# Two graph layers on one core: layer 2's probabilities turned by the transposing DMA instead of TensorE, and the gate completed on ScalarE

## What is computed

```python
# layer 1 (12 heads of 64)
h = einsum('bnd,ade->bane', x, W); th = tanh(h)
attn = leaky(th@w_src + swap(th@w_dst)); attn = softmax(where(adj, attn, -999))
f = elu(attn @ h + b)
gate = sigmoid(x @ H_w.T + H_b)
y = gate * f + (1 - gate) * x              # x = layernorm(x + y)
# layer 2 (6 heads of 128)
q, k, v = heads(x @ Wq + bq), heads(x @ Wk + bk), heads(x @ Wv + bv)
probs = softmax(q @ k.T / sqrt(128) + where(adj, 0, -9e15))
y = (probs @ v) @ Wf + bf                  # x = layernorm(x + y)
```

## Time and profile before

| | us |
|---|---|
| median of 3 runs | 2766.31 (2765.05 to 2766.51) |
| the profiled execution | 2766.33 |
| its span, first to last instruction | 2764.6 |
| between the two | 1.7 |
| mean granted TensorE clock | 0.997 |
| PE busy | 2726.9 (99%) |
| VectorE, ScalarE, GpSimd busy | 1668.8 (60%), 1160.3 (42%), 1066.3 (39%) |

### The profile page before, as it was taken

The page is one execution under the profiler, slowest core; times in us unless marked ns, Lnnn a source line. Parts: engine busy times, 40 slices in busy tenths (PEclk is TensorE's granted clock), DMA queues, the critical chain, the costliest instruction groups (busy, mean ns, idle before and its releaser), DMA issues.

```text
span 2764.6 us, 51821 instructions
## 1 busy us (share of the span) xinstructions
PE 2726.9 (99%) x20988; PEld 2517.8 (91%) x20988; DVE 1668.8 (60%) x3334; ACT 1160.3 (42%) x3045; POOL 1066.3 (39%) x630
## 2 busy tenths in 40 slices
PE   8999999999999989999999999999999999999998
PEld 6877778888788889999999999999999999999998
DVE  6888998888888754444454444454445445444443
ACT  5666776666666633322332233322332233223322
POOL 2453344433444134433444343434443343434340
PEclk9999999999999999999999999999999999999999
DMA  5656665555555512222213222222222222222220
GB/s 180 173 131 145 164 160 145 139 139 139 141 137 143 175 59 69 69 71 81 70 58 81 76 75 58 79 72 71 69 68 71 81 70 58 81 81 70 58 70 23
DMA packets 306894, 269.49 MB, mean 97 GB/s; under 512 B 227808, under 2 KB 244192, under 8 KB 306656
## 3 DMA queue, kind: packets, MB, share of 16 engines
q1 hardware_dynamic: 306656, 266.19, 35.5%
HBM read 142.65 MB, written 75.89 MB: 79 GB/s over the span
## 4 chain that ended last, share of the span: by engine, by line
PE 85%; DVE 5%; DMA 4%; issue 2%; POOL 2%; ACT 2%; SPq 1%; DVEq 0%; ACTq 0%; POOLq 0%
PE ps_hg L1036 21%; PE ps_a L1199 14%; PE ps_k L70 14%; PE ps_q L70 14%; PE ps_a L70 14%; PE ps_c L1165 2%; PE ps_s L1140 2%; PE ps_pv L1068 1%; DMA dst_all<-dst_scratch 1%; ACT logits L564 1%; PE ps_t L1055 1%; PE ps_pt L1165 1%; DMA dst_scratch<-dst 1%; PE ps_pt L1147 1%; DVE logits L770 1%
## 5 line engine op out<-in xcount | busy, mean ns | idle before, releaser
L1036 PE MATMUL ps_hg<-w_hi,xT 128*128 128x512 f32 x2268 | 745.6, 401 | 8.3 <-DVE h_one L803 8.2
L1036 PEld LDWEIGHTS ps_hg<-w_hi,xT 128*128 128x128 f32 x2268 | 426.1, 188 | 112.6 <-issue 11.3
L1036 PE MATMUL ps_hg<-w_lo,xT 128*128 128x512 f32 x1134 | 448.4, 395 | 0.0
L70 PE MATMUL ps_k<-x1T_hi,wk_hi 128*128 128x256 f32 x1152 | 329.1, 286 | 0.0
L70 PE MATMUL ps_q<-x1T_hi,wq_hi 128*128 128x256 f32 x1152 | 323.5, 281 | 1.4 <-DVE x1T_lo L910 1.4
L70 PE MATMUL ps_q<-x1T_lo,wq_hi 128*128 128x256 f32 x1152 | 322.6, 280 | 0.0
L70 PE MATMUL ps_k<-x1T_lo,wk_hi 128*128 128x256 f32 x1152 | 321.9, 279 | 0.0
L70 PE MATMUL ps_q<-x1T_hi,wq_lo 128*128 128x256 f32 x1152 | 321.9, 279 | 0.0
L70 PE MATMUL ps_k<-x1T_hi,wk_lo 128*128 128x256 f32 x1152 | 321.1, 279 | 0.0
L496 POOL TENSOR_TENSOR th_src<-th,wsrc_all 128x768 f32<-128x768 f32 x64 | 118.3, 1848 | 483.7 <-DVE dst_all L783 463.4
L648 ACT ACTIVATE qT<-ps_q,bq_col 128x256 f32<-128x256 f32 x192 | 80.5, 470 | 479.3 <-PE ps_q L70 479.3
(11 more groups left out here) (144 smaller groups left out, 5814.2 us busy)
## 6 DMA issues: line engine op xcount, KB each, us to landing
x_tok<-x SPq DMA_DIRECT2D x64, 384.0 KB, 4.1
dst_all<-dst_scratch SPq DMA_DIRECT2D x128, 192.0 KB, 3.4
gate_scratch<-gate SPq DMA_DIRECT2D x64, 384.0 KB, 2.6
feat_scratch<-feat SPq DMA_DIRECT2D x128, 192.0 KB, 2.8
feat_in<-feat_scratch SPq DMA_DIRECT2D x62, 384.0 KB, 3.1
gate_in<-gate_scratch SPq DMA_DIRECT2D x62, 384.0 KB, 3.7
x_even<-x SPq DMA_DIRECT2D x16, 768.0 KB, 4.2
x_odd<-x SPq DMA_DIRECT2D x16, 768.0 KB, 4.4
```

The lines of the kernel that those rows point to most:

```text
L70: ins = pe.matmul(out, left[a][c], right[b][c], start=(n == 0), stop=(n == len(terms) - 1))
L1036: ins = pe.matmul(ps_hg[:, cols], left[a][c], right[b][c], start=(c == 0 and n == 0), stop=(c == KC - 1 and n == 2))
```

## The change

For groups 2 to 31 the two PE transposes of each pair are gone. Instead:

- GpSimd splits the pair's probabilities (128 x 256 words) into two 16-bit planes of 128 x 256 (`split_p1`), behind `times_gate` of tile t for pairs 0 and 1, and after both for pair 2.
- SyncE issues one DMA transpose per pair (`turn_p1`, four 128 x 128 blocks of 16 bits), for pair 0 between the load of x and the load of feat_in and gate_in of t = 1, for pairs 1 and 2 behind that.
- ScalarE and VectorE take over the diagonal blocks and join the planes in one step (`join_block`, two copies each of 64 x 256 16-bit elements), now from SBUF.
- `logits_of` waits for the split of the pair before it, and `scores` for the logits of the pair before it.

The gate is completed by one ScalarE activation per tile, 0.5 g + 0.5 (`whole_gate`), in place of GpSimd's addition of 1; the mix takes 2 x instead of 4 x, and its eps EPS instead of 4 EPS. The places of `whole_gate`: behind `k_out(G, 0)` and `q_out(G, 2)`; in group 0 behind `exps(0, 0)` and behind the three chunks of weights. On VectorE, from group 2 on, `rstd_start` stands ahead of the logits of pair 2, `probs_out(G, 1)` and `rstd_end` behind them and ahead of `normalise(G, 2)`, and `probs_out(G, 2)` ahead of `context_lo(G, 0)`. On ScalarE `probs_out(G, 1)` goes behind `exps(G, 2)`.

```diff
@@ -193,6 +193,8 @@
         bf_all = at(S + 55232, "bf_all", [P, D])
+        planes_p1 = at(S + 53184, "planes_p1", [P, 2, PN * NODES], U16)
+        planes_p1T = at(S + 54208, "planes_p1T", [P, 2, 2, P], U16)
         x1_tok = [x_even, x_odd]
@@ -242,6 +244,7 @@
         turned1 = [sem(f"turned1_{t}") for t in range(GT)]
+        split_p1_done, turned_p1 = (sem(n) for n in ("split_p1_done", "turned_p1"))
         v_done, v_copied, o_done, o_added = (sem(n) for n in ("v_done", "v_copied", "o_done", "o_added"))
@@ -262,6 +265,15 @@
             copy(out_, src_).then_inc(signal, 1)
+        def join_block(copy, buf, t, g, signal):
+            s = graph(g)
+            out_ = probs1T[s, buf, :, s].bitcast(U16).rearrange("p (h t) (n l) -> p l h t n", t=GT, l=2)[:, :, :, t, :]
+            copy(out_, planes_p1T[t * NODES:(t + 1) * NODES, :, :, s]).then_inc(signal, 1)
+        def pair_of(G, j):
+            return PAIRS * (G - BY_DMA) + j + 1
@@ -423,6 +435,13 @@
+            def turn_p1(G, j):
+                sp.wait_ge(split_p1_done, pair_of(G, j))
+                for joined_ in (ptc_act, ptc_dve):
+                    sp.wait_ge(joined_, 2 * (PAIRS * G + j))
+                sp.dma_start_transpose(planes_p1T.rearrange("p l h n -> p (l h) n"),
+                                       planes_p1.rearrange("p l (h m) -> p (l h) m", h=2)).then_inc(turned_p1, 16)
             for G in range(NG):
@@ -441,8 +460,14 @@
                     sp.dma_start(x1_tok[s][:, :, :], x_g[G + 2]).then_inc(x1_in[s], 16)
+                if BY_DMA <= G + 1 < NG:
+                    turn_p1(G + 1, 0)
+                if G + 2 < NG:
                     sp.wait_ge(mixed, GT * (G + 2) + 1)
                     feat_and_gate(G + 2, 1)
+                if BY_DMA <= G + 1 < NG:
+                    for j in range(1, PAIRS):
+                        turn_p1(G + 1, j)
             for s in range(2):
@@ -478,7 +503,6 @@
                 pool.wait_ge(delta_done, GT * G + t + 1)
-                pool.tensor_scalar(gate_, gate_, 1.0, None, ALU.add).then_inc(gate_ready, 1)
                 pool.wait_ge(gate_ready, GT * G + t + 1)
@@ -520,6 +544,13 @@
+            def split_p1(G, j):
+                pool.wait_ge(probs_done, PAIRS * G + j + 1)
+                if pair_of(G, j) > 1:
+                    pool.wait_ge(turned_p1, 16 * (pair_of(G, j) - 1))
+                pool.tensor_copy(planes_p1[:, :, :], scores_sb.rearrange("p k m -> p (k m)").bitcast(U16)
+                                 .rearrange("p (d l) -> p l d", l=2)).then_inc(split_p1_done, 1)
             for G in range(NG):
@@ -534,10 +565,14 @@
                         join_x1(G, t)
-                if 1 <= G < NG - 1:
-                    for t in range(GT):
+                for t in range(GT):
+                    if 1 <= G < NG - 1:
                         feat_less_x(G + 1, t, feat_in[:, :])
                         times_gate(G + 1, t, feat_in[:, :], gate_in[:, :])
+                    if G >= BY_DMA:
+                        split_p1(G, t)
+                if G >= BY_DMA:
+                    split_p1(G, GT)
@@ -604,6 +639,13 @@
                 act.activation(feat[:, :], feat[:, :], ACT.Exp, scale=-1.0).then_inc(eexp_done, 1)
+            def whole_gate(G, t, gate_):
+                if G == 0:
+                    act.wait_ge(fg_first[t], 32)
+                else:
+                    act.wait_ge(fg_in, 32 * (GT * (G - 1) + t + 1))
+                act.activation(gate_, gate_, ACT.Copy, scale=0.5, bias=0.5).then_inc(gate_ready, 1)
@@ -627,6 +669,9 @@
                     elu_exp(T - 2)
+                for t in range(GT):
+                    if T == MIX + 2 * t:
+                        whole_gate(0, t, gate_first[:, t, :])
                 if PREFETCH < T <= PREFETCH + EARLY_W1 - LATE_W1:
@@ -675,9 +720,14 @@
             def probs_out(G, j):
-                act.wait_ge(pt1_done, PAIRS * G + j + 1)
-                for g in range(2):
-                    copy_block(act.copy, (G + j) % 2, 0, g, ptc_act)
+                if G < BY_DMA:
+                    act.wait_ge(pt1_done, PAIRS * G + j + 1)
+                    for g in range(2):
+                        copy_block(act.copy, (G + j) % 2, 0, g, ptc_act)
+                else:
+                    act.wait_ge(turned_p1, 16 * pair_of(G, j))
+                    for g in range(2):
+                        join_block(act.copy, (G + j) % 2, 0, g, ptc_act)
@@ -706,10 +756,16 @@
                     k_out(G, 0)
+                    if G + 1 < NG:
+                        whole_gate(G + 1, 0, gate_in[:, :])
                 q_out(G, 1)
                 exps(G, 0)
+                if G == 0:
+                    whole_gate(1, 0, gate_in[:, :])
                 k_out(G, 1)
                 q_out(G, 2)
+                if 1 <= G < NG - 1:
+                    whole_gate(G + 1, 1, gate_in[:, :])
                 if G == 0:
@@ -722,13 +778,17 @@
                 value_out(G, 0)
-                probs_out(G, 1)
+                if G < BY_DMA:
+                    probs_out(G, 1)
                 exps(G, 2)
+                if G >= BY_DMA:
+                    probs_out(G, 1)
                 value_out(G, 1)
...
                         w1_round(act, EARLY_W1 + n)
+                    whole_gate(1, 1, gate_in[:, :])
                     act.wait_ge(feat_stored, 32 * NT)
@@ -840,7 +900,7 @@
                 dve.wait_ge(gated_done, GT * G + t + 1)
-                dve.scalar_tensor_tensor(out=x_, in0=x_, scalar=4.0, in1=feat_, op0=ALU.mult,
+                dve.scalar_tensor_tensor(out=x_, in0=x_, scalar=2.0, in1=feat_, op0=ALU.mult,
                                          op1=ALU.add).then_inc(mixed, 1)
@@ -893,7 +953,7 @@
                     input_moments(0)
-                    rstd_start(in_newton, 0, 4 * EPS)
+                    rstd_start(in_newton, 0, EPS)
                 elif T == MIX + 2 * GT + 2:
@@ -914,8 +974,10 @@
                     dve.wait_ge(bias_mask, G + 1)
+                elif G < BY_DMA:
+                    dve.wait_ge(pt1_done, PAIRS * G + j)
                 else:
-                    dve.wait_ge(pt1_done, PAIRS * G + j)
+                    dve.wait_ge(split_p1_done, pair_of(G, j - 1))
                 dve.scalar_tensor_tensor(
@@ -932,9 +994,16 @@
             def probs_out(G, j):
-                dve.wait_ge(pt1_done, PAIRS * G + j + 1)
-                for g in range(2):
-                    copy_block(dve.tensor_copy, (G + j) % 2, 1, g, ptc_dve)
+                if G < BY_DMA:
+                    dve.wait_ge(pt1_done, PAIRS * G + j + 1)
+                    for g in range(2):
+                        copy_block(dve.tensor_copy, (G + j) % 2, 1, g, ptc_dve)
+                else:
+                    dve.wait_ge(turned_p1, 16 * pair_of(G, j))
+                    if j == 2:
+                        dve.wait_ge(c_done, PAIRS * G + 1)
+                    for g in range(2):
+                        join_block(dve.tensor_copy, (G + j) % 2, 1, g, ptc_dve)
@@ -973,20 +1042,32 @@
                     input_moments(G + 1)
-                probs_out(G, 1)
+                    if G >= BY_DMA:
+                        rstd_start(in_newton, G + 1, EPS)
+                if G < BY_DMA:
+                    probs_out(G, 1)
                 logits_of(G, 2)
-                if 1 <= G < NG - 1:
-                    rstd_start(in_newton, G + 1, 4 * EPS)
+                if G >= BY_DMA:
+                    probs_out(G, 1)
+                elif G >= 1:
+                    rstd_start(in_newton, G + 1, EPS)
+                if BY_DMA <= G < NG - 1:
+                    rstd_end(in_newton, G + 1)
                 normalise(G, 2)
...
                     input_moments(1)
-                    rstd_start(in_newton, 1, 4 * EPS)
+                    rstd_start(in_newton, 1, EPS)
+                if G < BY_DMA:
+                    rstd_end(in_newton, G + 1)
                 if G + 1 < NG:
-                    rstd_end(in_newton, G + 1)
                     input_norm(G + 1)
-                context_lo(G, 0)
-                probs_out(G, 2)
+                if G < BY_DMA:
+                    context_lo(G, 0)
+                    probs_out(G, 2)
+                else:
+                    probs_out(G, 2)
+                    context_lo(G, 0)
                 if G == 0:
@@ -1130,6 +1211,8 @@
             def scores(G, j):
+                if G >= BY_DMA:
+                    pe.wait_ge(logit_done, PAIRS * G + j)
                 pe.wait_ge(q_copied, 2 * (PAIRS * G + j + 1))
@@ -1235,18 +1318,21 @@
                 query(G, 2)
-                transpose_probs1(G, 0)
+                if G < BY_DMA:
+                    transpose_probs1(G, 0)
                 scores(G, 1)
...
                 value(G, 0)
-                transpose_probs1(G, 1)
+                if G < BY_DMA:
+                    transpose_probs1(G, 1)
                 scores(G, 2)
...
                 first_context(G)
-                transpose_probs1(G, 2)
```

(2 more changed lines are left out.)

## The result

| | before | after |
|---|---|---|
| median of 4 runs each, us | 2765.68 (2764.57 to 2766.51) | 2827.44 (2818.32 to 2832.79) |
| ratio, with its 95% interval | | 1.022 (1.019 to 1.025) |
| the profiled execution, us | 2766.33 | 2818.32 |
| its span, us | 2764.6 | 2816.6 |
| mean granted TensorE clock | 0.997 | 0.991 |

Slower by 62 us, where 12 less were forecast. One execution of the last experiment (e12) took 3332.89 us at a mean granted clock of 0.751, and its ratio leaves it out. First the page of the changed kernel: the rows that answer to the earlier trace rows, and the chain by engine; the last line is that of the kernel before.

The account below looks back on a forecast made before the run. TensorE, busy 99% of the span, was taken as the bound. -19.8 for transposes, +3.6 for group 0 and +4 for late groups gave -12.2, so 2754 us; own range 2746 to 2760, 8-in-10 range 2745 to 2795.

Parts of the forecast that it names:

- Copies of pair 2 on VectorE, now from SBUF: Behind the transpose's landing: 0.62 us, bounds 0.5 and 0.85; with c_lo of pair 0 (0.88) done at 2179.8.
- the road to the deadline: Steps from pair 0's division to c_lo of pair 0, ahead of last_contexts at 2180.08: slack 0.3 us.
- GpSimd holds VectorE's copies: Rival, 22%: copies within SBUF wait out GpSimd's split and bias addition; stall 1.7 us per group, 2805 us.
- charge for late groups: Seven of 30 groups, 0.6 to 1.5 us late by late loads, lose about 0.7 each; 4 us charged.
- The transposes: Leaving TensorE in 30 groups x 3 pairs at 0.22 us: 19.8 us saved, nothing hidden.
- worth less: Rival, 8%: TensorE's transposes cost less than 0.22 us each; at half, 9.9 us less gain, 2764.
- Landing and queue: The new DMA transpose: lands 2.75 us after issue (bounds 2.2 and 4.0), holds SyncE's queue 0.6 us.
- long-landing rival: 17%: landing of 3.6 to 4.0 us stalls TensorE 0.6 to 0.9 us per group; 2776 to 2785 us.
- The split: GpSimd's split of a pair's probabilities: 0.6 us, bounds 0.5 and 1.46; pair 0's meets the mix and runs behind it.
- Group 0: Gate of t = 1 behind three weight chunks on ScalarE moves the chain by 3.6 us of TensorE waiting; bounds 1.0 and 4.5.
- Layer 1: Its two gate tiles (T = 8 and 10) cost nothing, as ScalarE has room beside a busy TensorE.

Follow-up runs that it names:

- e12: Kernel before, with one edit: GpSimd's addition of 1 to the gate written as tensor_scalar with two operations; 2760.31 us, ratio 0.9977.
- e1: Changed kernel, but GpSimd waits with the next input's splits until VectorE has copied pair 2; 2757.66 us, ratio 0.9963.
- e4: Changed kernel, but VectorE takes pair 2 over with a tensor_reduce in place of a copy; 2759.54 us, ratio 0.9974.
- e3: Changed kernel, but pair 2 goes back to TensorE's transposes, with c_lo of pair 0 ahead of its copies; 2753.61 us, ratio 0.9952.
- e6: Changed kernel with GpSimd's splits waiting for pair 2's copies, c_lo of pair 0 ahead of them, group 0's second gate ahead of weight chunks; 2745.87 us.

## Why the prediction was wrong

**The step that failed** is "Copies of pair 2 on VectorE, now from SBUF: 0.62, bounds 0.5 and 0.85 for twice the elements". They took 2.7 us, outside the bounds, because GpSimd held them (e1 and e4), and TensorE waited 51.6 us for the c_lo behind them where the forecast had no wait. All the rest of the road to the deadline came out in time or ahead; against the group's start:

| step | forecast | after |
|---|---|---|
| second mix starts | 27.8 | 27.8 |
| logits of pair 2 start | 31.8 | 31.7 |
| split of pair 2 ends | 36.5 | 36.0 |
| its transpose has landed | 39.3 | 38.4 |
| the two copies end | 39.9 | 41.2 |
| c_lo of pair 0 ends | 40.9 | 42.1 |
| deadline | 41.1 | 41.1, TensorE starts at 42.4 |

VectorE's timeline of the changed kernel, from which the first rows come:

```profile
2143.08 0.95 DVE L903 SCALAR_TENSOR_TENSOR x_odd<-x_odd,feat_in 128x768 f32<-128x768 f32 x1
...
2147.03 0.42 DVE L981 SCALAR_TENSOR_TENSOR scores_sb<-ps_s,mask 128x256 f32<-128x256 f32 x1
...
2153.77 2.71 DVE L272 COPY probs1T<-planes_p1T 64x256 uint16<-64x256 uint16 x2 [2.05 <-DMA planes_p1T<-planes_p]
2156.51 0.88 DVE L1012 SCALAR_TENSOR_TENSOR cT_lo<-ps_c,bv_col,cT_hi 128x256 fp32r<-128x256 f32 x2
```

- **The rival "GpSimd holds VectorE's copies"** had the mechanism, with the engines, the two instructions waited for and their order. It put the stall at 1.7 us against a deadline that had moved forward by 0.66; the usual gaps were 1.0 to 1.6, since the landing came 0.8 earlier. I gave it 22% because "neither is a copy with one input held by GpSimd". That was true of the rows. Yet the rule of the Trainium skill cited beside that rival names copies, and nothing in the trace spoke against it: c_lo has an input in PSUM and so is no evidence.
- **That rival's 2805 was still short of 2827**, by the charge for late groups and by the clock. I charged 4 us for late groups; in nine of 29 the gap was 2.4 us and more (up to 4.2). I had also read the late groups of the kernel before as less late than they are: the group of the earlier trace rows is itself 56.48 us long, so its second mix came 1.7 us late against its own start and not 1.27, and the latest of all 2.1. And nothing in my sum let TensorE's clock fall behind a gap (13.7 us in the profiled execution, the fastest of the four) or charged the restart behind one (7.0).
- **The transposes** were worth what was forecast. e3 saves two thirds of 19.8, wins 4.6 in layer 1 and loses 3.5 in group 0 and 0.3 in gaps: -14.0; measured -13.5. e6 saves all, wins 2.2 in layer 1 and loses 1.4 in group 0: -19.8 - 2.2 + 1.4 = -20.6; measured -21.3. The rival "worth less" is out.
- **Landing and queue.** Landing 2.4 where 2.75 stood and the long-landing rival wanted 3.6 to 4.0. SyncE's queue was held 1.20 us, not 0.6: a third of the blocks costs 80% of the 1.49. The loads behind it paid 0.5 us for that.
- **The split** takes 0.60 alone, as forecast, but 1.27 beside the mix and 1.00 beside `input_norm`, whose two take 1.56 in place of 1.27. It starts at once beside the mix, where I had let it wait, so the end is nearly the same.
- **Group 0**: forecast 3.6, and TensorE's wait grew by 3.5 (9.2 against 5.6); the output product starts 4.1 us later against the group's start. **Layer 1** was costed at nothing and gave 4 back; that the two cancel is luck. I had asked whether ScalarE has room for the gate tiles, and not what GpSimd's two additions had been costing.

## What to carry to other kernels

When an edit moves an operand of a VectorE copy from PSUM to SBUF, look at what GpSimd does at that time: price the copy to the end of GpSimd's instruction, once for each copy, since GpSimd takes the next turn. If that lands on a deadline, move the copy, the GpSimd work, or write it as a reduction; each of the three was worth 36 to 70 us here. Add to each stall the restart behind it (0.24 us here) and the time that TensorE may then run at its lower clock (here behind seven of the 12 gaps of 1.96 us and more, 2 us lost each time on average), and read what an instruction costs on the engine that it leaves as closely as on the one to which it goes.

## What the runs showed of the hardware that I had not expected

- GpSimd's `tensor_scalar` on 128 x 768 floats in place takes 2.14 us with one operation (plus 1) and 0.83 with two (times 1, plus 1): 62 instructions each, before and in e12.
- GpSimd wins the turn between two VectorE copies that stand right behind each other: in 27 of the 29 groups the two took 2.68 to 2.73 us together, the end of one GpSimd instruction and the whole of the next.
- A transpose of four blocks of 128 x 128 holds SyncE's queue for 1.20 us and lands after 2.4; one of twelve blocks 1.49 and 4.0.
